# A Perceiver-like network on one core: the tail of a query-softmax layer in another order, score offsets by one-column matmuls, and the next cross attention with its scores 12 chunks ahead and its exponentials in quarters

## What is computed

```python
# L0_ffn: attention with its softmax over the queries, two l2 norms, gelu
attn = jax.nn.softmax(scores, axis=-1)          # scores[b, k, q]
z = out.reshape(B, H, S, dh).transpose(0, 2, 1, 3).reshape(B, S, L)
z = _l2_normalize(z @ Wo)
z = _l2_normalize(z @ Wff)
z = jax.nn.gelu(z, approximate=False)
# L1_xattn: cross attention with one head over the context
q = query @ Wq + bq; k = key @ Wk + bk; v = value @ Wv + bv
attn = jax.nn.softmax(einsum('bqe,bke->bqk', q, k), axis=-1)
out = einsum('bqk,bke->bqe', attn, v)
```

## Time and profile before

| | |
|---|---|
| runs | 1521.42, 1521.95, 1525.59 us; median 1521.95 |
| profiled execution | 1524.63 us, of which the span of the instructions 1522.8 |
| granted TensorE clock over the span | 0.978 of full speed |
| busy: PE, PEld (weight loads) | 1417.0 us (93%), 834.9 us (55%) |
| busy: DVE, ACT, POOL | 1077.9 us (71%), 920.7 us (60%), 290.3 us (19%) |
| chain that ended last | PE 71%, ACT 10%, DVE 10%, issue 4%, DMA 2% |
| the stage in question | first score at 1101.9 us, last weighing ends at about 1275 us |

### The profile page before, as it was taken

How to read it: one execution, slowest core, us unless ns; L and a number is a source line. 1 busy time by engine, 2 the same in 40 slices (tenths; PEclk the granted TensorE clock), 3 DMA queues, 4 the chain that set the end, 5 groups by cost and what they waited for, 6 DMA issues and landing times.

```text
span 1522.8 us, 28221 instructions
## 1 busy us (share of the span) xinstructions
PE 1417.0 (93%) x11142; PEld 834.9 (55%) x11142; DVE 1077.9 (71%) x2222; ACT 920.7 (60%) x1895; POOL 290.3 (19%) x331
## 2 busy tenths in 40 slices
PE   7799999999999999999999998899878998888898
PEld 4355555555555555555455544545446667745565
DVE  5787777787777787777888864667666557757657
ACT  5366776777777776776777773257743442437721
POOL 3363222222222221222210003000120001220110
PEclk9799999999999999999999999999989999989999
DMA  6965653555644466545453405030013201166000
GB/s 190 163 144 134 116 120 81 103 120 115 126 108 86 90 126 127 121 98 91 95 105 57 70 1 184 1 111 1 22 56 104 63 1 52 32 132 119 2 0 28
DMA packets 95588, 133.13 MB, mean 87 GB/s; under 512 B 8864, under 2 KB 70944, under 8 KB 89504
## 3 DMA queue, kind: packets, MB, share of 16 engines
q1 hardware_dynamic: 95456, 131.33, 40.1%
HBM read 94.08 MB, written 37.22 MB: 86 GB/s over the span
## 4 chain that ended last, share of the span: by engine, by line
PE 71%; ACT 10%; DVE 10%; issue 4%; DMA 2%; POOL 1%; SPq 1%; DVEq 0%; ACTq 0%; POOLq 0%
PE psum L545 16%; PE psum L526 13%; PE psum L510 12%; ACT probs L765 4%; PE psum L573 3%; PE psum L270 3%; PE psum L1857 3%; PE psum L612 2%; PE psum L1839 2%; PE psum L2496 2%; DVE peaks L669 2%; PE psum L1432 1%; PE psum L279 1%; PE psum L2506 1%; PE psum L2121 1%
## 5 line engine op out<-in xcount | busy, mean ns | idle before, releaser
L669 DVE TENSOR_REDUCE peaks<-psum 128x1 f32<-128x512 f32 x1024 | 641.7, 684 | 194.5 <-PE psum L510 194.2
L765 ACT ACTIVATE probs<-psum 128x512 f32<-128x512 f32 x1024 | 525.5, 617 | 67.0 <-PE psum L526 63.2
L526 PE MATMUL psum<-queriesT,keysT 98*128 98x256 bf16 x2048 | 394.0, 274 | 8.0 <-ACT queriesT L828 3.1
L510 PE MATMUL psum<-keysT,queriesT 96*128 96x512 bf16 x1024 | 390.2, 384 | 10.6 <-DMA keysT<-key_parts 7.2
L526 PEld LDWEIGHTS psum<-queriesT,keysT 98*128 98x128 bf16 x2048 | 173.3, 99 | 202.1 <-ACT probs L765 81.8
L545 PE MATMUL psum<-probs,values 128*17 128x256 f32 x4096 | 245.9, 380 | 1.1 <-ACT probs L765 1.1
L545 PEld LDWEIGHTS psum<-probs,values 128*17 128x17 f32 x4096 | 107.2, 97 | 103.7 <-issue 26.8
L510 PEld LDWEIGHTS psum<-keysT,queriesT 96*128 96x128 bf16 x1024 | 98.6, 97 | 84.2 <-issue 52.7
L896 POOL CAST key_parts<-key_f 128x512 bf16<-128x512 f32 x57 | 34.8, 610 | 517.0 <-ACT key_f L798 509.4
L798 ACT ACTIVATE key_f<-psum,bk 128x512 f32<-128x512 f32 x59 | 40.5, 687 | 118.8 <-PE psum L573 118.7
L1885 DVE TENSOR_REDUCE peaks<-row_w 128x1 f32<-128x512 f32 x64 | 43.3, 681 | 60.6 <-ACT row_w L1941 60.6
(11 more groups left out here) (297 smaller groups left out, 1710.1 us busy)
## 6 DMA issues: line engine op xcount, KB each, us to landing
keysT<-key_parts SPq DMA_DIRECT2D x31, 768.0 KB, 7.7
key_parts<-key_parts SPq DMA_DIRECT2D x90, 256.0 KB
keysT<-key_parts SPq DMA_DIRECT2D x31, 512.0 KB, 10.0
ctx_nat<-in_ctx_dram SPq DMA_DIRECT2D x32, 256.0 KB, 4.3
keysT<-key_parts SPq DMA_DIRECT2D x31, 256.0 KB, 11.5
ctx_in<-in_ctx_dram SPq DMA_DIRECT2D x24, 256.0 KB, 6.0
ctx_turned<-ctxT SPq DMA_DIRECT2D x24, 256.0 KB, 4.3
ctx_T<-ctx_turned SPq DMA_DIRECT2D x12, 512.0 KB, 4.6
```

The costliest lines, as they stand in the source:

```text
L510: e.matmul(ps, self.queriesT[0:ROWS, u % 2, g * GH + j, t * P:(t + 1) * P], self.keysT[0:ROWS, i % RING, j, c * BANK:(c + 1) * BANK], star ...
L526: made = e.matmul(ps[:, j * S:(j + 1) * S], self.keysT[0:AUG, i % RING, j, kt * P:(kt + 1) * P], self.queriesT[0:AUG, u % 2, g * GH + j, : ...
L669: e.tensor_reduce(self.peaks[:, i % 2, pair, c:c + 1], k.ps(("max", n)), AX.X, ALU.max).then_inc(*self.peaked.up(n))
L765: e.activation(self.probs[:, t % RINGP, e2 * GH * S:(e2 + 1) * GH * S], k.ps(("scores", t, e2)), ACT.Exp).then_inc(*self.exped.up((t, e2)))
```

## The change

1. Offsets: `offset` becomes a job of TensorE, eight matmuls with one moving column per half (`xnT` is loaded as weights), and VectorE only adds a column. The folded bias shrinks from 257 to 3 columns.
2. Schedule of the query-softmax tail: products 4 to 7 are in slots 36, 36, 37, 37 behind the last weighting of values, context chunks 4 to 7 are turned in slots 40, 40, 43, 43 and no longer in 36, and half 1's jobs come 2 to 4 slots later.
3. Cross attention: AHEAD is 12; peaks are taken one step behind the score, and behind the copy of the turned chunk and `ucT`; exponentials are in quarters of 1024 columns, one in each of four steps, between copies; the turning of weights is in steps -3 to -1.

```diff
-    LATE = PAIRS3 + 30
+    LATE = PAIRS3 + 31
...
-        for t, slot in enumerate((14, 16, 22, 23, 35, 35, 37, 37)):
+        for t, slot in enumerate((14, 16, 22, 23, 36, 36, 37, 37)):
...
-        for c, slot in enumerate((33, 33, 34, 34, 36, 36, 36, 36)):
+        for c, slot in enumerate((33, 33, 34, 34, 40, 40, 43, 43)):
...
-                (26, 31, (37, 38), 38, 39, (40, 40), 45), (43, 44, (48, 49), 52, 54, (56, 57), 60))):
+                (26, 31, (37, 37), 38, 39, (41, 41), 45), (46, 47, (50, 51), 54, 57, (59, 60), 62))):
...
+            elif job == "offset":
+                half, = a
+                ps = bank(("offset", half), (self.offset_made, ("offset", half)))
+                w.wait_ge(self.folded, ("fold", "bias"))
+                for i in range(4):
+                    t = 4 * half + i
+                    for kk in range(KD):
+                        w.wait_ge(*self.turned(half, kk))
+                        made = e.matmul(ps[:, i:i + 1], l.xnT[:, kk, t * P:(t + 1) * P], l.folded[:, D + 1 + kk:D + 2 + kk],
+                                        start=(kk == 0), stop=(kk == KD - 1))
...
-    AHEAD = CH + 3
+    AHEAD, QUARTERS = CH + 4, 4
...
             if 0 <= s - 2:
                 yield ("weigh",) + divmod(s - 2, CH)
-            if 1 <= s < 4:
-                yield "turn weights", s - 1
+            if 0 <= n - 1 < NT * CH:
+                yield ("peak",) + divmod(n - 1, CH)
+            t, quarter = divmod(n - CH - 1, CH)
+            if 0 <= t < NT and quarter < self.QUARTERS:
+                yield "exponentials", t, quarter
+            if -3 <= s < 0:
+                yield "turn weights", s + 3
...
-                w.wait_ge(self.exped, (t, 2 * c // CH))
+                w.wait_ge(self.exped, (t, self.QUARTERS * c // CH))
...
-                for half in range(2):
-                    own = slice(half * LC // 2, (half + 1) * LC // 2)
-                    e.activation(self.row_w[:, r, own], self.row_w[:, r, own], ACT.Exp, bias=self.stat[:, t, 2:3],
-                                 accum_out=self.stat[:, t, 3 + half:4 + half]).then_inc(*self.exped.up((t, half)))
+                e.activation(self.row_w[:, t % 2, own], self.row_w[:, t % 2, own], ACT.Exp, bias=self.stat[:, t, 2:3],
+                             accum_out=self.stat[:, t, 3 + quarter:4 + quarter]).then_inc(*self.exped.up((t, quarter)))
```

More of the change, by code:

```diff
@@ L1531, in tensor_slot @@
                 made.then_inc(*k.projected.up(("qc", b)))
+            elif job == "offset":
[4 more added lines that the diff above has]
+                    t = 4 * half + i
+                    for kk in range(KD):
+                        w.wait_ge(*self.turned(half, kk))
+                        made = e.matmul(ps[:, i:i + 1], l.xnT[:, kk, t * P:(t + 1) * P], l.folded[:, D + 1 + kk:D + 2 + kk],
+                                        start=(kk == 0), stop=(kk == KD - 1))
+                made.then_inc(*k.projected.up(("offset", half)))
     def keep_columns(self, e, w, name, half, m, engine):
@@ L1628, in vector_slot @@
                 else:
-                    e.tensor_copy(l.folded[:, D + 1:2 * D + 2], ps[:, 0:D + 1]).then_inc(*self.folded.up(("fold", name)))
+                    e.tensor_copy(l.folded[:, D + 1:D + 2 + KD], ps[:, 0:KD + 1]).then_inc(*self.folded.up(("fold", name)))
             elif job == "products" and a[0] < 4:
@@ L1881, in vector @@
             r = t % 2
-            if job == "score":
+            if job == "peak":
                 here = slice(c * BANK, (c + 1) * BANK)
```

47 lines of the change are left out of this document (20 added, 27 removed).

## The result

| | before | changed kernel |
|---|---|---|
| runs of one session (7 each) | 1521.42 to 1528.14 us, median 1524.89 | 1503.88 to 1512.70 us, median **1511.38** |
| ratio to before | | 0.990, 95% interval 0.9873 to 0.9927 |
| profiled execution (span) | 1524.63 us (1522.8) | 1503.98 us (1502.2) |
| mean granted clock of it | 0.978 | 0.984 |

The median is outside the range of 1495 to 1509. Profiled execution against profiled execution the gain is 20.6 us, where the sum said 21.2; median against median it is 13.5. The changed kernel's executions lie in two groups: 1503.88, 1503.98 and 1504.94 us with a mean clock of 0.983 to 0.984, and four of 1511.38 to 1512.70 with 0.974 to 0.975. The profile shown is one of the first group, and that has to be remembered in reading it.

What follows compares the result with a forecast made beforehand. The prediction took the stage to be bound by TensorE, but for waits and its slow-clocked start. Its terms, -3.7 - 8.8 - 7.0 - 2.5 + 0.8 = -21.2, carried 1521.95 to 1501 us, range 1495 to 1509.

Steps and rivals of the forecast that it cites:

- Up to score 0: Query-softmax tail before the first cross-attention score: score 0 moves from 1101.9 to 1098.2, -3.7 us.
- Score 0 to score 16: Start of the cross attention: 25.2 us instead of 37.0, with 3.0 of work still to do, -8.8 us.
- Exponentials: Cross attention, six tile changes: quarters instead of two halves in a row remove wait and refill, -7.0 us.
- ucT: Bank of a finished tile, five tiles: loss falls from 1.13 to 0.63 us each, -2.5 us.
- Offsets of half 1: Cross attention: a weighing's wait of 1.7 us with refill goes, 2.5 us on TensorE come, +0.8 us.
- terms 1 to 5: The five parts of the forecast in order: -3.7, -8.8, -7.0, -2.5 and +0.8 us, sum -21.2.
- the last one: Carrying the sum to the whole kernel: later stages move with this stage's end, 1521.95 - 21 = 1501 us.
- a sign of being wrong: After the stage: a later stage that starts 21 us earlier and ends less than that earlier.
- terms 2 and 5: The parts from score 0 to score 16 (-8.8 us) and for half 1's offsets (+0.8), each counting 2.5 of loads.
- My rivals: Four other outcomes: late start 1507 us (chance 0.21), fewer waits 1496 (0.09), new waits 1518 (0.04), slower 1527 (0.02).
- given back: Cross attention: filled slots meet a new 2 us wait at every tile change, 1518 us; chance 0.04.

Runs made afterwards that it cites:

- twice: The changed kernel with every offset matmul made twice (same column written again): 1514.61 us, ratio 0.9928 to the kernel before.
- late_norm: The changed kernel with `xn` of half 1 and its dependent jobs four slots later, behind the first chunk copies: 1505.29 us, ratio 0.9859.
- halves: The changed kernel with exponentials again in two halves in a row, all else changed: 1510.28 us, ratio 0.9896.
- lead_only: The changed kernel with peaks and exponentials (two halves) placed as before, scores still 12 ahead: 1524.78 us, ratio 0.9975.
- peak_first: The changed kernel with every peak again in its score's step, ahead of the chunk copy and `ucT` copy: 1508.90 us, ratio 0.99.
- offset_dve: The changed kernel with offsets and folded bias as before (offsets on VectorE), all else changed: 1500.18 us, ratio 0.9835.
- before_a: The kernel before, without any edit, run again for a second profile: 1525.73 us.
- wide: The changed kernel with its one-column matmuls made 128 columns wide, same number of weight loads: 1507.71 us, ratio 0.9882.

## Why the prediction was right and wrong

**Up to score 0** (forecast -3.7): 4.0 by the start stretch. Right. Score 0 stood at 1097.3 for 1098.2, the remaining 0.7 being differences upstream.

**Score 0 to score 16** (forecast 25.2 us): 1122.54 - 1097.30 = 25.2. Right in sum, by two errors against each other. The 16 loads of the offsets took 1.70 us (1100.97 to 1102.67), not 2.5. I had weighed the Trainium skill's rule (TensorE: Matmul & The Clock Gate, section "LDWEIGHTS (loading the stationary operand)", 107 ns for 128 columns) against a row of four loads, and let the row decide. That row was 0.63 us in length, modelled end included, and not a distance between starts; the rule's 1.7 is what was measured, and twice shows it again. The other way, `xn` of half 1 took 3.31 us and not 1.38 to 2.33, so that weighing 0 waited 2.66 where I had 2. It ran wholly beside GpSimd's eight additions (6.82 us from 1113.41); in late_norm it took 2.33 us, beside additions in its later part only. The Trainium skill (Advanced Engine Details and Errata, section "VectorE Performance Modes") says that VectorE's second SBUF port is shared with GpSimd, and that GpSimd and VectorE's two-port instructions block each other, which agrees; no run here takes the additions away by themselves.

**Exponentials** (-7.0): the size is right (18.17 us from tile to tile, forecast 18.2; no wait for `col_w` behind weighing 0). The cause is not: quarters brought 1.1 us (halves), none of it at the tile changes. My sentence was that copies, peaks and turned chunks "were late behind" the halves, and I put all of it down to their length. What held the chunk copy was a peak ahead of it on VectorE, which waited for a score copy behind shift and both halves. The change cuts that chain at three places (peak behind the copy, exponentials two copies later, quarters); undoing the first or the last alone does not bring the wait back, undoing all three does (lead_only, stage 16.1 us longer, with what stands at its start and two stretches of lowered clock). They share one gain, and the forecast gave it to one of them. How much the later start does by itself stays open, so that the size of the term came out right for a reason that it did not have: that is luck. A quarter took 1.14 us for 1.06, which nothing waited for.

**`ucT`** (-2.5): waits of 0.38 to 0.4 where I had 0.52; peak_first brings 0.9 back. Right, also in its cause.

**Offsets of half 1** (+0.8): 1.7 us of loads for 1.7 us of wait, so about 0. The move is not needed for it either: in the new order VectorE's offsets held no weighing there (offset_dve).

So start and stage gained 22.1 us where terms 1 to 5 said 21.2. **The step that failed is the last one**: "the later stages are tied to this one's end and move with it. 1521.95 - 21 = 1501". Both halves of it failed.

*They do not move with it.* The rest became 2.1 us longer, a sign of being wrong that the prediction named itself. The offsets' move was costed as the loads of terms 2 and 5 alone; what its two bank takes do to later layers was put at nothing without a reason. The runs show a new wait of 1.0 to 1.4 us in the last layer in each of the 13 profiles with offsets on TensorE (0.8 us of the 2.1), and a lower clock near the end (1.2), whose cause is open. With the offsets on VectorE and all else changed the rest is 236.9 and the median 1500.18 (offset_dve): the forecast time, but of a kernel without that part of the change. That the profiled gain is 20.6 for 21.2 is in part luck: the rest's loss and 1.0 us ahead of the head pairs stand against 1.6 us of head pairs that were short by chance and 0.9 us more in start and stage.

*The time that it was carried to.* Of the miss of 10.4 us 0.4 are the sum (21 for 20.6). Then, 1521.95 was a median of three; that of seven is 1524.89, and no later session's was under 1524.65: 2.9 us. The remaining 7.1 us are the changed kernel's own spread: the sum is one execution's, and the gain is 20.6 us between profiles and 13.5 between medians, since over half of the changed kernel's executions are of the group with the lower clock. The profiles of that group show where: 5 to 6 us in the head pairs, 1.5 to 1.7 behind weighing 0's wait. That the head-pair part comes by chance in both kernels is shown by before_a; that it hits the changed kernel's median more is only counted, not explained.

My rivals had no case for this. All were about the stage; the clock was read there alone, and the three runs of before with a spread of 4 us and its mean clock of 0.978 were not taken as a sign that a median carries more than its profile. The sum of *given back* counts its wait of 2 us once, though it is to come at every tile change; nothing hung on it.

## What to carry to other kernels

- An in-order engine is held by the first instruction that isn't ready, not by the longest: look which instruction waits ahead of the late one, and what that one waits for. Edits that cut one chain of waits at several places share one gain, and must not be added.
- A forecast from one profiled execution needs a term for the spread of executions: read the granted clock in the stages that aren't touched too, and profile the same kernel more than once before carrying a difference to a median.
- Where one counter hands out buffers to all layers, a job that takes one more shifts them for every later layer: look behind the changed place for waits with a new releaser, before a stage is called untouched.
- Take the price of a small instruction from distances between starts in a row of them, not from the length of a short group.

## What the runs showed of the hardware

- The same code, waiting the same 2.48 us, then ran its 40 matmuls in 5.47 or 8.10 us, by the clock granted (1.00 or a mean of 0.58). The changed kernel's executions lay some 8 us apart by this (1504 us at a mean clock of 0.984, 1512 at 0.975). The Trainium skill (TensorE: Matmul & The Clock Gate, section "What's actually happening") calls the slow matmuls of a kernel's start run-variable. The traces agree on the varying, but here the clock falls again in the middle of the kernel too, mostly right behind a wait of TensorE (0.72 us at 1016 in before, 2.48 at 1424 and 3.32 at 1259 in the changed kernel), and the same wait does not bring it each time.
- One-column matmuls in 32 bits cost 0.106 to 0.11 us a row (the profile shows two rows for each), as much as turning 128 columns (0.11). Made 128 columns wide (`wide`), 16 rows took 1.78 us for 1.70, so the columns that move do not set the price. That the load of weights does is the reading that fits, and was not tried by itself.
- Four scalings of 128x256 by VectorE took 1.38 us alone, 2.33 partly and 3.31 us wholly beside GpSimd's additions.
